# Conv passes: each block of eight gathers starts only when the one before it has landed

## The reference

```python
out = relu(n_feat @ lin0_w.T + lin0_b)
eh = relu(e_feat @ en1_w.T + en1_b)              # one row of 128 per edge, the same in all steps
w_e = (eh @ en2_w.T + en2_b).reshape(-1, D, D)   # D = 32
for _ in range(6):
    msg = einsum('ei,eio->eo', out[src], w_e)
    agg = segment_sum(msg, dst, num_segments=n_nodes) + conv_bias
    h = out = gru_cell(relu(agg), h)
```

## Time and profile before

| what | us |
|---|---|
| median of 3 runs | 24027.48 |
| span of the profiled execution | 30532.6 |
| first gather of the first conv pass | 9973.8 |
| last gather of the sixth conv pass | 29305.6 |
| POOL busy | 14020.9 |
| PE busy | 18622.1 |

### The profile page before, as it was taken

The page is one execution under the profiler, slowest core; times in us unless marked ns, Lnnn a source line. Parts: engine busy times, 40 slices in busy tenths (PEclk is TensorE's granted clock), DMA queues, the critical chain, the costliest instruction groups (busy, mean ns, idle before and its releaser), DMA issues. The chain is left out here.

```text
span 30532.6 us, 420576 instructions
## 1 busy us (share of the span) xinstructions
PE 18622.1 (61%) x121575; PEld 13266.8 (43%) x121575; DVE 11720.7 (38%) x29589; ACT 7911.3 (26%) x20853; POOL 14020.9 (46%) x16639
## 2 busy tenths in 40 slices
PE   3333555555655676667666766676666766676654
PEld 3333322222244454455444554455445544554444
DVE  5444566666710333233323333233323332333220
ACT  0000344445510222222222322232222222232210
POOL 4886355555610444534453445344443445344520
PEclk5555788888977777777777877787777777787777
DMA  3222233322278222112211221122112221122147
GB/s 97 48 49 69 85 122 118 113 99 93 68 293 344 66 64 59 52 58 65 58 54 53 68 63 55 48 69 63 56 53 60 63 59 54 57 65 60 55 142 308
DMA packets 1398480, 2692.30 MB, mean 88 GB/s; under 512 B 938471, under 2 KB 1104704, under 8 KB 1189106
## 3 DMA queue, kind: packets, MB, share of 16 engines
q10 hardware_dynamic: 335568, 1445.71, 13.4%
q1 hardware_dynamic: 709952, 1053.68, 10.0%
q0 software_dynamic: 352256, 186.21, 4.3%
HBM read 2105.10 MB, written 1242.55 MB: 110 GB/s over the span
## 5 line engine op out<-in xcount | busy, mean ns | idle before, releaser
L785 POOL DMA_INDIRECT sb_xg<-node_rows,sb_src_c x9408 | 8876.9, 944 | 11917.8 <-SPq L803 6579.1
L921 PE MATMUL banks<-sb_work,sb_eh_sb 128*128 128x256 f32 x29184 | 8833.9, 453 | 1693.7 <-issue 1358.2
L921 PEld LDWEIGHTS banks<-sb_work,sb_eh_sb 128*128 128x128 f32 x29184 | 6472.3, 229 | 3674.0 <-issue 2259.6
L874 DVE TENSOR_TENSOR sb_work<-sb_xs,banks_p 128x2048 f32<-128x2048 f32 x1824 | 4171.1, 2288 | 9843.7 <-remote 5895.0
L978 ACT ACTIVATE sb_work<-banks 128x512 f32<-128x512 f32 x7296 | 4124.9, 599 | 11185.0 <-remote 7003.8
L1200 PE MATMUL banks<-sb_hot_code,sb_xs 128*128 128x392 bf16 x7296 | 1874.5, 371 | 2173.7 <-DVE sb_work L1163 1435.1
L1163 DVE SCALAR_TENSOR_TENSOR sb_work<-sb_work,sb_eh_sb,banks 128x784 f32 x2432 | 2502.3, 1029 | 572.4 <-PE banks L1202 484.1
L864 DVE COPY sb_xs<-sb_xg 128x32 f32 x14592 | 1762.7, 191 | 2459.9 <-issue 2268.6
L907 PE MATMUL banks_p<-sb_work,sb_en 128*32 128x256 f32 x29184 | 2084.7, 391 | 778.6 <-issue 766.1
L367 POOL DMA_INDIRECT slots<-sb_rows,sb_slot_u x1600 | 2108.6, 1318 | 786.7 <-issue 762.6
L1079 POOL TENSOR_SCALAR sb_xs<-sb_codes,sb_code 128x128 bf16<-128x128 f16 x2432 | 1516.6, 624 | 2067.3 <-PE banks L1202 2067.1
(11 more groups left out here) (281 smaller groups left out, 13084.1 us busy)
## 6 DMA issues: line engine op xcount, KB each, us to landing
sb_eh_sb<-eh ACTq DMA_DIRECT2D x912, 1024.0 KB
weights_between<-sb_work ACTq DMA_DIRECT2D x305, 1568.0 KB
edges_between<-sb_work ACTq DMA_DIRECT2D x305, 1568.0 KB
sb_work<-weights_between SPq DMA_DIRECT2D x147, 3136.0 KB, 12.5
sb_work<-edges_between SPq DMA_DIRECT2D x98, 3136.0 KB, 12.4
eh<-sb_eh_sb ACTq DMA_DIRECT2D x304, 512.0 KB, 2.6
sb_xg<-node_rows,sb_src_c POOLq DMA_INDIRECT x9408
sb_win_row<-window_rows SPq DMA_DIRECT2D x100, 488.3 KB
```

The source lines that it names most:

```text
L785: nc.gpsimd.indirect_dma_start(m.xg_ring[:, row % RING * D:(row % RING + 1) * D], None, m.node_dram, bass.IndirectOffsetOnAxis(ap=m.src_c[ ...
L874: V.tensor_tensor(m.spread[q], m.xs[h].rearrange("s (t i) -> s t i", i=D)[:, tiles, :].unsqueeze(3) .broadcast_to([P, TS, D, WN]), m.mask_ ...
L921: o = mm(m.ps_pair[u % 4][:, v, :, :], m.eh[h % 2][:, t * K:(t + 1) * K], m.spread[t // TS][:, t % TS, :, :], start=True, stop=True)
```

## The change

From block 1 on, every block also waits until all eight gathers of its predecessor have landed: 16 x 8 more on the predecessor's `got` semaphore. The wait for `room` stays as it is. The wait of blocks 4 to 7 for `landed` goes, since the new one is stricter.

```diff
         if b >= RING // JC:
             pool.wait_ge(room, b - RING // JC + 1)
             hold(pool, held)
-        elif b >= L:
-            pool.wait_ge(landed, b - L + 1)
+        if b >= 1:
+            pool.wait_ge(got[(b - 1) % L], ((b - 1) // L + 1) * 16 * JC)
             hold(pool, held)
         for t in range(JC):
             row = b * JC + t
```

## The result

The changed kernel takes 26325.06 us (median of four runs, 26320.83 to 26329.75); the kernel before took 24024.13 beside it (four runs, 24020.3 to 24047.04). The ratio is 1.0957, with a 95% interval from 1.0941 to 1.0972: slower by 2301 us. The forecast was 25,850, slower.

The account below looks back on a forecast made before the run. POOL's issuing was taken to bound the conv passes. Outside 12,275 us plus six passes of 2305 (1960 + 195 x 1.77) gave 26,105; with outside 11,775, 25,605; the middle, 25,850, was forecast, own range 25,170 to 26,375, whole range 24,300 to 26,450.

Parts of the forecast that it names:

- The ring nearly empty: Conv passes, timed runs: the ring has room, so the room wait takes none of the 1.77 us added per block.
- 1960 met 1959: Each conv pass: POOL's 1568 gathers at 1.25 us give 1960 us; the timed median less the outside gives 1959.
- The outside: Time outside the six passes' gather stretches: 12,275 us, or 11,775 if 500 us of setup waits are missing from timed runs.
- The pause: POOL at each block end, 195 a pass: 2.07 us in place of 0.30, so 1.77 us more.
- restart: Part of POOL's block-end wait: from release to the next gather's start, 0.77 us.
- landing: Part of POOL's block-end wait: from POOL's end of the last gather to the block seen landed, 1.30 us.
- Inner gaps unchanged at 0.30: Between gathers inside a block, POOL's gap stays at 0.30 us in the new profile.
- a thing of the profiled execution that the timed runs lack: Conv-pass stalls with gathers in flight, ACT's 7003.8 us, belong to profiling; the profile is 6505 us longer than timed runs.
- A: Consumers set the pace in timed runs too, the pause lies under 817 room waits: 24,030 us; chance 0.08.
- B: POOL issues faster in timed runs, say 1.0 us a gather; only dense parts pay 860 us: 24,890; chance 0.13.
- C: Pauses break up stalls in the passes, winning 1170 us against 860 given back: 23,720 us; chance 0.07.
- D: Longer waits keep TensorE at its lower clock in sparse halves of passes, 1410 us more: 27,260; chance 0.05.

Follow-up runs that it names:

- 3: Changed kernel, but only odd blocks wait for their direct predecessor, even ones for the block two back: 25251.37 us, ratio 1.0511.
- 4: Changed kernel, with each block's fifth gather also waiting for the first four gathers of its block to land: 29113.62 us, ratio 1.2116.
- 7: Changed kernel, but each block waits for only the first seven gathers of its predecessor, on their own semaphores: 25364.01 us, ratio 1.0558.
- 8: Kernel before, with two POOL memsets of an unused tile ahead of each block but the first, no added landing wait: 24605.64 us, ratio 1.024.
- 5: Kernel before, with 8 of the 32 products with `en2` left in each batch, so less work for PE: 23785.98 us, ratio 0.99.
- experiment 1: Kernel before, profiled once more with its two waits written as two ifs, the same instructions: 24036.75 us in its profiled execution.
- 12: Kernel before with a ring of 128 places; blocks from 4 on wait for block b - 4 on its own semaphore: 23798.9 us, ratio 0.9905.
- Experiment 11: Changed kernel, with the 1 MB `eh` load that ScalarE issues for each batch cut to a sixteenth: 26125.43 us, ratio 1.0866.
- 2: Kernel before, with each block waiting for the landing of the block two back, on the transfers' semaphore: 24023.75 us, ratio 0.9995.
- 6: Kernel before, with the changed kernel's predecessor wait moved to ahead of each block's fifth gather: 24015.24 us, ratio 0.9995.
- 9: Kernel before with a ring of 128 places instead of 64; blocks from 4 on wait for `landed` of block b - 4: 23974.54 us, ratio 0.9974.
- 10: Changed kernel with a ring of 128 places instead of 64: 26239.47 us, ratio 1.0917.

## Why the prediction was right

**The bound.** Right, and shown: POOL's issuing sets the conv passes. Waits that POOL stops for and memsets come out in the time in full (3, 4, 7, 8), while 1033 us less for PE win 241 (5). "The ring nearly empty" was not quite so: experiment 1 still had 269 us of room waits, and experiments 5 and 12 won these and no more. That 1960 met 1959 so closely was luck: a pass of experiment 1 takes 1999.8.

**The outside.** The middle of two values, 12,025 us, was taken since the 500 us of unnamed setup waits could go either way. Measured: 12,036 in experiment 1 and 12,033 after. The term holds, by luck: nothing spoke for the middle over either end, 250 us away.

**The pause.** This is the term that was mis-sized: 2.07 us at each block end forecast, 2.31 measured. Its restart was right: by the semaphore records of the trace after, POOL goes on 0.77 us after the last update of the landing in 1152 of the 1170 block ends. Its landing was too short: 1.30 forecast, while that last update comes 1.54 us behind POOL's end on average (median 1.43; the last packet is there after 1.11, median). The 1.30 was read from a single block. Its row gives tenths, and the 9984.9 is 9984.95 in the trace. And its two `eh` loads had their last packets at 9981.05, before the block's last gather; beside a load that has just been issued the landing takes longer. Experiment 11, with smaller loads, has 1.36 on average and takes 200 us back. Times 6 x 195 the 0.24 is 281 us.

**Inside blocks.** "Inner gaps unchanged at 0.30" holds nearly. From 2381 us a pass the pauses' 451 and the gathers' 1568 x 0.948 = 1486 leave 444 for 1372 inner gaps, 0.32 each. Sixteen in a pass are long ones, as in this row of after's timeline:

```profile
10289.76 0.94 POOL L785 DMA_INDIRECT sb_xg<-node_rows,sb_src_c  x1 [1.86 <-issue]
```

With the gathers' 948 for 944 ns that is 2381 - 2305 - 47 = 29 us a pass, 175 in six. The long gaps stand at the same places in all six passes (ahead of the second gather of blocks 14, 26, 38 and so on, every twelfth), 16 a pass in experiment 11 too and four in experiment 1; so they go with a place in POOL's program and not with the loads, and their cause is open. Together, 281 + 175 + 8 for the outside make 464 of the 475 us by which the forecast was short; the rest is the 6 us around the span and rounding.

**The profiled execution.** Wrong: the new span was expected within some 600 us of the old 30,533, and it is 26,319. The step that failed is "a thing of the profiled execution that the timed runs lack", taken to mean that any profile would show the stalls. That they are absent from the timed runs was right, and it is what made the sum against the median work. But thirteen later profiles show none, so the rule from the page "NOTIFIC — the notification-queue block" of the Trainium skill, which the prediction set beside that step, finds no support in these runs; neither can they say what stalled that one execution. The forecast would have been 24,030 had it followed that trace's rows of waits.

**The rivals.** A (no change): refuted by the time, and experiment 1 shows that the 817 room waits were not those of a normal execution. B (POOL issues faster in timed runs): a gather takes 945 ns in an execution of 24036.75 us, and the loss is the full one, not 900 us. C (pauses break up stalls): experiment 1 shows no stalls to break. D (the clock) fell as a cost, though its premise came true. The two stretches of the first pass, of experiment 1 and of after (length, busy time and count by engine, granted clock, DMA share, GB/s):

```profile
9974.00:11975.00 2001.00, 1743.49 (x11400) 1364.27 (x11400) 1037.09 (x3030) 893.37 (x2035) 1481.95 (x1568) 0.89 0.33 94
```

```profile
9968.00:12350.00 2382.00, 1839.66 (x11400) 1436.01 (x11400) 1029.82 (x3030) 892.52 (x2035) 1486.90 (x1568) 0.83 0.27 79
```

The granted clock, a mix of 1.2 and 2.4 GHz, fell from 0.89 to 0.83, and PE was busy 96 us longer with the same matmuls. PE has 542 us to spare in that pass, so the longer time is covered there: POOL's stretch of 2381 us sets the pass.

**What would show it.** 1152 waits for the landing, three for room, DVE's waits for line 800 from 2669.8 us (experiment 1) to 6549.4: all as named, with the inner gaps nearly so.

## What to carry to other kernels

Where the engine that issues the transfers is the bound, a wait that is met on arrival costs nothing (experiments 2 and 6), and a wait that it stops for costs the landing and the restart in full (here 1.54 and 0.77 us on average), however much stock lies in the ring; so move the wait a few issues later, or ask for an older transfer. Have it ask the transfer's own semaphore rather than a count that another engine raises in its own order (12 against 9: 176 us). And when the span of a profile and the timed runs differ by a quarter, work out each stage against the timed median before believing the rows of waits, or profile again.

## What the runs showed that was not expected

- POOL goes on 0.77 us after the last update of the semaphore that it stops for (median), in the changed kernel and in experiments 3, 4, 7, 10 and 11 alike. The update comes some 0.3 us after the last packet: 1.43 against 1.11 us behind POOL's end (after, medians).
- The last packet of a gather of 128 rows, 1.1 us behind POOL's end, comes after 2.8 us beside a 1 MB load that another queue has just begun (after, 24 cases), and after 1.1 beside one of 64 KB (experiment 11).
- A few gaps between gathers of a block are long, at the same places of POOL's program in every pass: 16 a pass after, four in experiment 1, none in experiment 3.
- One execution of the kernel before held 7003.8 us of stalls that no other profile of this case shows.
